# State-space stage of a two-layer decoder: three of four channel blocks summed by accumulating transposes, and a third block convolved on TensorE

## The chip, the cores and the metric

One core of one Trainium2 chip runs the whole program. Its engines are TensorE (PE in the profile, PEld its weight loads), VectorE (DVE), ScalarE (ACT), GpSimd (POOL) and SyncE (SP), which issues the DMAs. The metric is the device time of one launch in microseconds (us), the median over runs.

## What is computed

A decoder of two layers over 8 sequences of 100 tokens and 256 channels. Layer 0 is a gated scan, cross attention and a mixture of experts; layer 1 is four state-space blocks, cross attention and a quantised feed-forward. The change touches the state-space blocks alone. One of the four is, cut:

```python
h = rms(x, norm_w[i])
xz = einsum('bld,ed->ble', h, W_in[i]);  xi, z = split(xz, 2)         # 512 channels each
xc = silu(conv_b[i] + sum(xp[:, k:k + L] * conv_w[i][:, k] for k in range(4)))
dbc = einsum('bld,ed->ble', xc, W_x[i]);  delta, Bm, Cm = split(dbc)
delta = softplus(einsum('blr,dr->bld', delta, W_dt[i]) + b_dt[i])
deltaA = exp(delta[..., None] * A);  BX = (delta * xc)[..., None] * Bm[:, :, None, :]
hs = scan(deltaA, BX)                                                 # 16 states per channel
y = einsum('bldn,bln->bld', hs, Cm) + D[i] * xc
x = x + einsum('bld,ed->ble', y * silu(z), W_out[i])
```

## The kernel before

The state-space stage works in 8 rounds (`ROUNDS`), one for each of 4 blocks and each of 2 groups of four sequences (`GT` = 400 tokens). The 512 channels lie as four blocks c = 0 to 3 of 128 partitions (`CD`), and the 16 states come four at a time, so a round has 16 units (`UNITS`): unit u is block u // 4 and states 4 (u % 4) to 4 (u % 4) + 3, a tile of 128 x 1600. A unit passes through the engines so:

- GpSimd multiplies dx by the rows of B (`gm_bx`, L2003), two units ahead, into one of three buffers.
- ScalarE takes the exponentials of a half unit (128 x 800) into one of two PSUM halves (`am_unit`, L1886). The half that it writes must have been consumed two halves before.
- VectorE scans each half. For eleven units of a round (`DVE_C`) it scans in PSUM (L2089) and multiplies by the rows of C itself (L2092). For units 1, 2, 6, 9 and 12 it scans into SBUF (L2094), and GpSimd multiplies by C (`gm_c`, L2015).
- TensorE adds the four states of a unit onto the sum of the block, four fp32 matmuls with the identity (`pm_reduce`, recorded under the helper's line L675), two units later (`LAG_R`); after the fourth unit of a block one more adds D times xc. The sums lie in banks 4 and 5. VectorE multiplies a block's sum by silu(z) (`vm_y`, L2110).

Between the units, each engine's program holds the side work for the next round, at places given in units by the table `AT`; a piece at u stands behind unit u of its engine. TensorE: output projection of the round before (`pO`), transposes (`pT`, L1547), input projections X0 to X7 (`pX`), convolution of blocks 2 and 3 (`pm_conv`), the product DB (`pB`), steps D0 to D3 (`pD`). ScalarE: squares and scales for the norm (L1756, L1776), copies of T, X, Y, DB (L1787, L1801, L1807, L1825, L1845), the taps as scaled identities for the TensorE convolution in every second round (`am_taps`, L1816), softplus (L1852) and silu (L1835, L1840) with table loads around (L670). VectorE: convolution of blocks 0 and 1 (`vm_conv`, L2052), three steps each. GpSimd: delta (L1992) and the norm's root (L1953 to L1960).

The results of the side work use PSUM banks 6 and 7 in turn, in the order of the list `PREP`; each waits until the one two places before it has been read. Every engine's program is in order, with semaphore waits written by hand. The last round has no next one to prepare; pieces of the following attention stand in it as guests.

Of the kernel before, what the change touches and what calls it, by code (L numbers as in the profile page):

```python
# [17 lines left out]
P = 128  # L18
# [10 lines left out]
G = 2  # L29
# [70 lines left out]
    "aK": 2,  # L100
    "aQ": 4,
    "gN": 4,
    "aH": 5,
    "pT": 7,
    "aT": 6,
    "pX": (9, 9, 8, 8, 15, 15, 16, 16),
    "aG": (5, 6),
    "aX": 7,
    "aY": 8,
    "aC": 9,  # L110
    "vC": 10,
    "aZ": (15, 15, 16, 16),
    "aV": 3,
    "aS": 11,
    "pB": 11,
    "aB": 12,
    "pD": (12, 12, 14, 14),
    "aD": (13, 14),
    "aA": 10,
    "gA": 15,  # L120
    "gD": (14, 15, 19, 21),
    "vY": (5, 10, 13, 16),
# [110 lines left out]
def decoder(nc, inp, out):  # L233
    ctx = ExitStack()
    with ctx:
# [62 lines left out]
        taps = mam.take(2, DC, P)  # L298
        mam.at += CD * GT - 2 * DC * P
        dx = mam.take(CD, GT)  # L300
        bx = mam.take(BX, SEGMENT * GT)
        hs = mam.take(HS, SEGMENT * GT)
        y2 = mam.take(CD, GT)
# [663 lines left out]
        def act_attn(act, a, steps):  # L967
            for g in steps:
# [11 lines left out]
                if a.layer == 0:  # L980
# [41 lines left out]
                    if g == AHEAD["aU"]:  # L1022
                        am_unit(act, 0)
# [372 lines left out]
        m_taps = sem("m_taps")  # L1396
        ROUNDS = G * NL


        PREP = (["T0", "T1", "X2", "X3", "Y2", "Y3", "X0", "X1", "DB"] + [f"D{c}" for c in range(CD)]  # L1400
# [47 lines left out]


# [111 lines left out]

        def pm_conv(pe, m, c):

            pe.wait_ge(m_taps, m // G + 1)
            n = f"Y{c}"
            p_read(pe, m, f"X{c}")
            p_free(pe, m, n)
            y3 = ps[:, p_bank(m, n), 0:GT].rearrange("p (b t) -> p b t", b=GB)
            x3 = xc[m % G][:, c].rearrange("p (b t) -> p b t", b=GB)
            for s in range(DC):  # L1570
                last = mm(y3[:, :, s:S], taps[:, c - 2, DC - 1 - s], x3[:, :, 0:S - s], s == 0, s == DC - 1)
            last.then_inc(m_full, 1)
# [16 lines left out]
        def pm_reduce(pe, unit):  # L1589
# [12 lines left out]
            last.then_inc(m_red, 1)  # L1602

# [71 lines left out]
        def mam_pe(pe):  # L1675
            for m in range(ROUNDS):
                for u in range(UNITS):
# [8 lines left out]
                    if m + 1 < ROUNDS:  # L1686
# [7 lines left out]
                        for e in (0, 1, *range(CD, 2 * CD)):  # L1694
                            if u == AT["pX"][e]:
                                pm_in(pe, m + 1, e)
                    if UNITS * m + u >= LAG_R:
                        pm_reduce(pe, UNITS * m + u - LAG_R)
                    if m + 1 < ROUNDS:
                        if u == AT["pB"]:  # L1700
                            pm_dbc(pe, m + 1)
                        for c in range(CD):
# [69 lines left out]
        def am_scale(act, m, g):  # L1772
# [5 lines left out]
            if m >= 2:  # L1778
                am_keep(act, m - 2, g, 0)
                am_keep(act, m - 2, g, 1)  # L1780
# [29 lines left out]
        def am_taps(act, m, l, c):  # L1810

            act.wait_ge(ld_w, 80 * (l + 1))
            if m and c == 2:
                p_full(act, m, "Y3")
            for k in range(DC):
                last = nc.scalar.activation(taps[:, c - 2, k], ident[:, :], ACT.Identity,  # L1816
                                            scale=cvw[:, DC * c + k:DC * c + k + 1])
            if c == 3:
                last.then_inc(m_taps, 1)
# [7 lines left out]
        def am_silu(act, m, g):  # L1827
# [4 lines left out]
            for names, c in ((("Y2", "Y3"), 2), (("X0", "X1"), 0)):  # L1832
# [35 lines left out]
        def am_unit(act, unit):  # L1868

            m, u = divmod(unit, UNITS)  # L1870
            c, nq = divmod(u, NQ)
            l, g = divmod(m, G)
            if nq == 0:
# [3 lines left out]
            for h in range(2):  # L1877
                k = 2 * unit + h
                if unit:
                    if on_dve(unit - 1):  # L1880
                        act.wait_ge(m_cmd, dve_halves(unit - 1, h))
                    else:
                        act.wait_ge(m_scan, k - 1)
                for j in range(2):
                    n = c * NS + nq * SEGMENT + 2 * h + j
                    last = nc.scalar.activation(psf[:, half_at(k) + j * GT:half_at(k) + (j + 1) * GT],  # L1886
                                                delta[g][:, c], ACT.Exp, scale=aneg[:, l % 2, n:n + 1])
                last.then_inc(m_exp, 1)

        def mam_act(act):  # L1890
            table(act, SET_EXP_LN)
            for m in range(ROUNDS):
                l, g = divmod(m, G)
                ng = 1 - g
                for u in range(UNITS):
                    if m or u:
                        am_unit(act, UNITS * m + u)
                    for c in range(CD):
                        if m and u == AT["aZ"][c] - UNITS:
                            am_z(act, m, g, c)  # L1900
                    if u == AT["aV"]:
                        table(act, SET_SILU)
                        am_silu_z(act, m, g)
                        table(act, SET_EXP_LN)
                    if u == AT["aK"] and g == 0:
                        am_skip(act, m, l)
                    if m + 1 == ROUNDS:
                        if u == AT["aH"]:
                            am_keep(act, m - 1, ng, 0)
                            am_keep(act, m - 1, ng, 1)  # L1910
                        guest_act(act, u)
                        continue
                    if u == AT["aQ"]:
                        am_square(act, m + 1, ng)
                    if u == AT["aH"]:
                        am_scale(act, m + 1, ng)
                    if u == AT["aT"]:
                        am_turned(act, m + 1)
                    for c in (2, 3):
                        if u == AT["aG"][c - 2] and (m == 0 or g == 1):  # L1920
                            am_taps(act, m, l + g, c)
                        if u == AT["aX"]:
                            am_raw_x(act, m + 1, ng, c)
                    for c in (2, 3):
                        if u == AT["aY"]:
                            am_conv_out(act, m + 1, ng, c)
                    for c in range(2):
                        if u == AT["aC"]:
                            am_conv(act, m + 1, ng, c)
                    for c in range(CD):  # L1930
                        if u == AT["aZ"][c]:
                            am_z(act, m + 1, ng, c)
                    if u == AT["aS"]:
                        table(act, SET_SILU)
                        am_silu(act, m + 1, ng)
                        table(act, SET_EXP_LN)
                    if u == AT["aB"]:
                        am_dbc(act, m + 1)
                    for k in range(2):
                        if u == AT["aD"][k]:  # L1940
                            table(act, SET_SOFTPLUS)
                            for c in (2 * k, 2 * k + 1):
                                am_soft(act, m + 1, ng, c)
                            table(act, SET_EXP_LN)
                    if u == AT["aA"] and g == 1:
                        am_rates(act, l + 1)
# [96 lines left out]
        def vm_conv(dve, m, g, c0):  # L2043

            dve.wait_ge(m_acc, 2 * m + CD)
            for s in range(1, DC):
                for c in (c0, c0 + 1):
                    n = f"X{c}"
                    a3 = xc[g][:, c].rearrange("p (b t) -> p b t", b=GB)[:, :, s:S]
# [601 lines left out]
```

## Time and profile before

| | |
|---|---|
| median of 3 runs | 1283.72 us (1283.09 to 1285.94) |
| profiled execution | 1284.21 us, its span 1282.5 us |
| mean granted TensorE clock | 0.955 |
| busy: PE, DVE, ACT, POOL | 1120.2, 1050.9, 824.7, 775.1 us |
| state-space stage, VectorE's first scan to its last y | 359 to 1058 us |
| starts of unit 4 (behind the silu of z) in the rounds from the third on | 556.32, 642.00, 728.85, 814.81, 901.34, 987.03 us |

The last line gives rounds of 85.7, 86.9, 86.0, 86.5 and 85.7 us. Rounds are counted from 0 in what follows; the even one that is read closely runs from 556.3 to 642.0. A line of the timeline has the start, the time to the last end, the engine, the source line, the operation and its shapes, how many instructions are merged, and in brackets the idle time before it and who ended it. Where the engine named had long been done, the wait was another.

### The profile page before, as it was taken

Reading aid. Unit: us, or ns where it says so; the run is one execution under the profiler, and the core shown is the slowest. Engines: PE = TensorE matmul, PEld = TensorE weight load, DVE = VectorE, ACT = ScalarE, POOL = GpSimd, SP = SyncE. Lnnn points to the kernel's source line nnn. Section 1 sums busy time; section 2 is a strip of 40 time slices with the busy share of each in tenths; the row PEclk is TensorE's granted clock in tenths of the full one; section 3 lists DMA queues with packets and bytes.
Section 4 is the critical chain, followed back from the end, with each engine's and each line's share of the span. In section 5 each row is a group of like instructions: output and inputs, shape, how many; then the busy total and the mean of one; then the engine's idle time right before and its main releaser. Section 6 shows DMA issues by size and latency. Waiting matters only on the chain.

```text
span 1282.5 us, 17476 instructions
## 1 busy us (share of the span) xinstructions
PE 1120.2 (87%) x5960; PEld 655.7 (51%) x5960; DVE 1050.9 (82%) x1642; ACT 824.7 (64%) x1816; POOL 775.1 (60%) x641
## 2 busy tenths in 40 slices
PE   7798888888859899999998999999989679999874
PEld 3455555444425454454554544545545336667643
DVE  4567777676598999999999999999999895776667
ACT  1455555655476776776777767867776436788863
POOL 6001111100379889899899898998998961554212
PEclk9899999998789999999999999999999899999988
DMA  7000002000330420501504206005033003010000
GB/s 212 13 13 13 13 13 73 2 1 3 126 120 1 179 73 0 207 17 44 207 1 144 79 1 241 11 12 195 17 123 115 1 1 101 18 34 18 2 2 26
DMA packets 22141, 79.13 MB, mean 62 GB/s; under 512 B 4935, under 2 KB 8847, under 8 KB 21138
## 3 DMA queue, kind: packets, MB, share of 16 engines
q1 hardware_dynamic: 22054, 78.02, 17.5%
q8 instruction: 48, 0.79, 0.3%
q14 instruction: 39, 0.32, 0.1%
HBM read 76.77 MB, written 1.24 MB: 61 GB/s over the span
## 4 chain that ended last, share of the span: by engine, by line
PE 31%; DVE 31%; POOL 22%; issue 7%; ACT 7%; DMA 1%; SPq 0%; DVEq 0%; POOLq 0%; ACTq 0%
PE ps L675 27%; DVE ps L2089 13%; POOL arena L2003 13%; POOL arena L2015 6%; DVE arena L2092 4%; PE ps L744 4%; DVE hstat L1213 2%; DVE arena L2094 2%; DVE arena L2052 2%; DVE arena L1189 1%; POOL arena L1992 1%; ACT ps L1886 1%; ACT arena L936 1%; DMA arena<-in_exb 1%; DVE arena L1179 1%
## 5 line engine op out<-in xcount | busy, mean ns | idle before, releaser
L675 PE MATMUL ps<-arena 128*32 128x100 f32 (+10 forms) x3330 | 513.2, 375 | 54.2 <-ACT arena L936 15.1
L2003 POOL TENSOR_TENSOR arena<-arena 128x1600 f32<-128x1600 f32 x128 | 456.8, 3584 | 30.9 <-DVE ps L2089 22.6
L675 PE MATMUL ps<-arena,ident 128*128 128x400 f32 x1024 | 381.8, 522 | 45.2 <-POOL arena L2015 35.7
L1886 ACT ACTIVATE ps<-arena 128x400 f32<-128x400 f32 x512 | 282.9, 590 | 187.4 <-DVE arena L2092 152.9
L675 PEld LDWEIGHTS ps<-arena 128*32 128x32 f32 (+7 forms) x3330 | 259.1, 143 | 276.5 <-issue 114.3
L2089 DVE TENSOR_TENSOR_SCAN ps<-ps,arena 128x800 f32<-128x800 f32 x176 | 320.8, 1822 | 20.6 <-ACT ps L1886 12.6
L675 PEld LDWEIGHTS ps<-arena,ident 128*128 128x128 f32 x1024 | 198.6, 198 | 210.4 <-POOL arena L2015 44.1
L642 POOL TENSOR_SCALAR stat<-stat 100x1 f32<-100x1 f32 (+1 forms) x44 | 8.5, 193 | 420.0 <-DVE stat L623 419.0
L2092 DVE TENSOR_TENSOR arena<-ps,arena 128x800 f32<-128x800 f32 x176 | 174.4, 991 | 6.0
L2015 POOL TENSOR_TENSOR arena<-arena 128x1600 f32<-128x1600 f32 x40 | 143.1, 3578 | 17.5 <-DVE arena L2094 17.5
L2094 DVE TENSOR_TENSOR_SCAN arena<-ps,arena 128x800 f32<-128x800 f32 x80 | 140.3, 1803 | 2.1 <-ACT ps L1886 1.4
L960 ACT ACTIVATE arena<-ps 128x400 f32<-128x400 f32 x192 | 89.8, 503 | 24.0 <-PE ps L744 23.0
L744 PE MATMUL ps<-ident,arena 100*128 100x100 f32 x768 | 93.2, 259 | 8.1 <-DVE arena L1337 3.6
L951 ACT ACTIVATE arena<-arena,hstat 100x361 f32<-100x361 f32 x128 | 74.9, 588 | 37.1 <-DVE hstat L1189 37.1
L1189 DVE CUSTOM_DVE_ANT_0 arena<-ps,arena 100x361 f32<-100x361 f32 x128 | 60.6, 530 | 44.0 <-PE ps L675 44.0
L936 ACT ACTIVATE arena<-ps,hstat 100x361 f32<-100x361 f32 x128 | 71.7, 562 | 35.7 <-DVE hstat L1213 35.6
L744 PEld LDWEIGHTS ps<-ident,arena 100*128 100x128 f32 x768 | 77.5, 144 | 27.4 <-issue 9.7
L670 ACT ACT_TABLE_LOAD x65 | 83.4, 1283 | 1.2
L1213 DVE TENSOR_REDUCE hstat<-ps 100x2 f32<-100x722 f32 x64 | 57.8, 905 | 26.0 <-PE ps L675 25.7
L675 PE MATMUL ps<-wv,arena 128*128 128x256 f32 (+1 forms) x192 | 53.9, 407 | 4.3 <-DVE arena L1159 3.4
L675 PE MATMUL ps<-arena,wk 128*128 128x361 f32 x128 | 50.4, 522 | 1.5 <-ACT xm L1768 0.8
L1020 ACT ACTIVATE arena<-ps 100x512 f32<-100x512 f32 x32 | 19.1, 598 | 45.7 <-PE ps L675 41.2
(199 smaller groups left out, 1025.2 us busy)
## 6 DMA issues: line engine op xcount, KB each, us to landing
arena<-bc_scratch SPq DMA_DIRECT2D x64, 800.0 KB, 6.5
arena<-in_ctxT SPq DMA_DIRECT2D x16, 361.0 KB, 4.3
arena<-in_w_in SPq DMA_DIRECT2D x4, 1024.0 KB, 4.9
arena<-in_expT SPq DMA_DIRECT2D x1, 2048.0 KB, 13.0
arena<-in_w_out SPq DMA_DIRECT2D x4, 512.0 KB, 3.3
arena<-in_mask SPq DMA_DIRECT2D x8, 141.0 KB
arena<-in_xT SPq DMA_DIRECT2D x2, 400.0 KB, 4.0
x_tok<-in_x_tok SPq DMA_DIRECT2D x1, 800.0 KB
```

What stands on the lines that cost most here:

```text
L670: act.add_instruction(mybir.InstLoadActFuncSet(name=nc.get_next_instruction_name(), act_func_set_id=which, engine=mybir.EngineType.Activat ...
L675: return nc.tensor.matmul(outp, lhsT, rhs, start=first, stop=last)
L744: last = nc.tensor.transpose(ps[:, a.bank(b, name), k * S:(k + 1) * S], a.es[0:S, (n * QUAD + i) % 8, kc * P:(kc + 1) * P], ident[0:S, 0:S])
L936: nc.scalar.activation(a.es[0:S, v % 8, 0:SK], ps[0:S, i, 0:SK], ACT.Exp, bias=hstat[0:S, n % 2, 0, i:i + 1], scale=1.0, accum_out=hstat[0 ...
L960: nc.scalar.activation(a.aT[:, n % 2, r * QUAD * S:(r + 1) * QUAD * S], ps[:, a.bank(b, name), 0:QUAD * S], ACT.Copy).then_inc(a.freed(b, ...
L1213: nc.vector.tensor_reduce(hstat[0:S, n % 2, 0, i:i + 2], ps[0:S, i:i + 2, 0:SK], AX.X, ALU.max, negate=True).then_inc(a.max_ready, 1)
L1886: last = nc.scalar.activation(psf[:, half_at(k) + j * GT:half_at(k) + (j + 1) * GT], delta[g][:, c], ACT.Exp, scale=aneg[:, l % 2, n:n + 1])
L2003: nc.gpsimd.tensor_tensor(bx[:, unit % BX].rearrange("p (j t) -> p j t", j=SEGMENT), bbc[:, nq].rearrange("p (j t) -> p j t", j=SEGMENT), ...
L2015: nc.gpsimd.tensor_tensor(h, h, cbc[:, nq], ALU.mult).then_inc(m_cmp, 1)
L2089: nc.vector.tensor_tensor_scan(a, a, bx[:, unit % BX, w], 0.0, ALU.mult, ALU.add).then_inc(m_scan, 1)
L2092: nc.vector.tensor_tensor(y, a, cbc[:, nq, w], ALU.mult).then_inc(m_cmd, 1)
L2094: nc.vector.tensor_tensor_scan(y, a, bx[:, unit % BX, w], 0.0, ALU.mult, ALU.add).then_inc(m_scan, 1)
```

## The change

- The sums of blocks 0, 1 and 2: a bank is cleared by one matmul of zeros (bf16), and then each of the 16 pieces (four states, four sequences, 128 channels x 100 tokens) is transposed onto it, accumulating, as 100 tokens x 128 channels. ScalarE copies the turned sum to SBUF (`am_turned_sums`), and `pm_back` puts D times xc and four transposes back into the same bank. Block 3 is summed as before.
- Block 1 is convolved on TensorE as well (raw copy, `pm_conv`, biased copy); VectorE keeps block 0, three instructions in place of six.
- Places: the programs of ScalarE and VectorE are now cut by half units. Old side work of ScalarE stays where it was (u is now u + 0.5). The copies of the turned sums (`aYT`), the taps (`aG`) and block 1's raw copy and output take places of their own. The y multiplies move from behind units 5, 10, 13 and 16 to 7.0, 11.5, 15.5 and 16.5. Steps D2 and D3 go ahead of the sum in their step on TensorE. The taps have three semaphore counts in place of one, and `am_keep` is called by itself.

```diff
-    "aG": (5, 6),
+    "aG": {2: 7.0, 3: 8.0, 1: 9.0},
     "pX": (9, 9, 8, 8, 15, 15, 16, 16),
-    "aX": 7, "aY": 8, "aC": 9, "vC": 10, "aS": 11, "aB": 12, "aD": (13, 14), "aA": 10,
+    "aX": 7.5, "aY": 8.5, "aR1": 9.5, "aC": 9.5, "vC": 10.5, "pY1": 10, "aY1": 10.5,
+    "aS": 11.5, "aB": 12.5, "aD": (13.5, 14.5), "aA": 10.0,
+    "aYT": (6.0, 10.5, 15.0),
+    "pY": (7, 11, 15),
+    "vY": (7.0, 11.5, 15.5, 16.5),
...
-        PREP = (["T0", "T1", "X2", "X3", "Y2", "Y3", "X0", "X1", "DB"] + [f"D{c}" for c in range(CD)]
+        PREP = (["T0", "T1", "X2", "X3", "Y2", "Y3", "X1", "X0", "Y1", "DB"] + [f"D{c}" for c in range(CD)]
...
+            if c < CD - 1:
+                if nq == 0:
+                    mm(ps[0:S, 4 + c % 2, :], identb[0:1, 1:S + 1],
+                       identb[0:1, :].rearrange("p (o t) -> p o t", o=1).to_broadcast([1, GB, P]), True, False)
+                for j in range(SEGMENT):
+                    for b in range(GB):
+                        last = nc.tensor.matmul(ps[0:S, 4 + c % 2, b * P:(b + 1) * P],
+                                                hs[:, unit % HS, j * GT + b * S:j * GT + (b + 1) * S], ident[:, :],
+                                                is_transpose=True, start=False,
+                                                stop=nq == NQ - 1 and j == SEGMENT - 1 and b == GB - 1)
+                last.then_inc(m_red, 1)
+                return
...
+        def pm_back(pe, m, c):
+
+            pe.wait_ge(m_yt, (CD - 1) * m + c + 1)
+            pe.wait_ge(m_skip, m // G + 1)
+            o = ps[:, 4 + c % 2, 0:GT]
+            mm(o, dgd[:, c], xc[m % G][:, c], True, False)
+            for b in range(GB):
+                last = nc.tensor.matmul(o[:, b * S:(b + 1) * S], turned_rows(c)[0:S, b * P:(b + 1) * P], ident[0:S, 0:S],
+                                        is_transpose=True, start=False, stop=b == GB - 1)
+            last.then_inc(m_yb, 1)
...
+        def am_turned_sums(act, m, c):
+
+            act.wait_ge(m_red, UNITS * m + NQ * (c + 1))
+            nc.scalar.activation(turned_rows(c)[0:S, :], ps[0:S, 4 + c % 2, :], ACT.Copy).then_inc(m_yt, 1)
...
+                        if u == AT["pY1"]:
+                            pm_conv(pe, m + 1, 1)
+                        for c in (2, 3):
+                            if u == AT["pD"][c]:
+                                pm_dt(pe, m + 1, c)
                     if UNITS * m + u >= LAG_R:
                         pm_reduce(pe, UNITS * m + u - LAG_R)
+                    for c in range(CD - 1):
+                        if u == AT["pY"][c]:
+                            pm_back(pe, m, c)
...
-        def vm_conv(dve, m, g, c0):
-            dve.wait_ge(m_acc, 2 * m + CD)
+        def vm_conv(dve, m, g):
+
+            dve.wait_ge(m_acc, m + CD)
+            n = "X0"
             for s in range(1, DC):
-                for c in (c0, c0 + 1):
...
+            if c < CD - 1:
+                dve.wait_ge(m_yb, (CD - 1) * m + c + 1)
+            else:
+                dve.wait_ge(m_red, UNITS * m + NQ * CD)
             nc.vector.tensor_tensor(y2[:, c], ps[:, 4 + c % 2, 0:GT], sz[g][:, c], ALU.mult).then_inc(m_y2, 1)
```

## Rows read from the trace of the kernel before

**Rows 1.** Windows: span, busy (instructions) of PE, PEld, DVE, ACT, POOL, PEclk, DMA.

```profile
470.00:556.00 86.00, 79.96 (x248) 44.70 (x247) 83.05 (x64) 64.30 (x123) 79.80 (x36) 0.98 0.23 83
556.00:642.00 86.00, 80.82 (x250) 45.29 (x249) 83.08 (x65) 61.98 (x112) 80.22 (x35) 0.98 0.26 94
```

**Rows 2.** Timeline of VectorE in an even round.

```profile
542.81 6.95 DVE L2094 TENSOR_TENSOR_SCAN arena<-ps,arena 128x800 f32<-128x800 f32 x4
...
571.48 1.83 DVE L2089 TENSOR_TENSOR_SCAN ps<-ps,arena 128x800 f32<-128x800 f32 x1
...
592.11 3.54 DVE L2052 SCALAR_TENSOR_TENSOR arena<-ps,arena 128x396 f32<-128x396 f32 x6
...
601.09 3.52 DVE L2094 TENSOR_TENSOR_SCAN arena<-ps,arena 128x800 f32<-128x800 f32 x2
...
610.05 0.57 DVE L2110 TENSOR_TENSOR arena<-ps,arena 128x400 f32<-128x400 f32 x1
...
616.58 1.83 DVE L2089 TENSOR_TENSOR_SCAN ps<-ps,arena 128x800 f32<-128x800 f32 x1 [0.24 <-POOL arena L2003]
...
627.99 0.57 DVE L2110 TENSOR_TENSOR arena<-ps,arena 128x400 f32<-128x400 f32 x1 [0.27 <-PE ps L675]
```

**Rows 3.** Timeline of GpSimd in the same round.

```profile
546.41 3.57 POOL L2015 TENSOR_TENSOR arena<-arena 128x1600 f32<-128x1600 f32 x1 [1.68 <-DVE arena L2094]
...
567.82 7.11 POOL L2003 TENSOR_TENSOR arena<-arena 128x1600 f32<-128x1600 f32 x2
...
592.54 7.14 POOL L2003 TENSOR_TENSOR arena<-arena 128x1600 f32<-128x1600 f32 x2
```

**Rows 4.** Timeline of ScalarE, same round, the exponentials behind the second softplus.

```profile
615.33 2.15 ACT L1886 ACTIVATE ps<-arena 128x400 f32<-128x400 f32 x4
```

**Rows 5.** Timeline of TensorE, same round.

```profile
584.00 2.85 PE L675 MATMUL ps<-arena,ident 128*128 128x400 f32 x8
...
592.65 4.62 PE L675 MATMUL ps<-arena,ident 128*128 128x400 f32 x8 [2.44 <-POOL arena L2015]
...
613.58 2.95 PE L675 MATMUL ps<-arena 128*128 128x400 f32 x8 [0.70 <-ACT arena L1852]
...
621.75 5.54 PE L675 MATMUL ps<-arena,ident 128*128 128x400 f32 x16
627.12 0.83 PE L675 MATMUL ps<-arena 128*128 128x400 f32 x2
```

**Rows 6.** Timeline of VectorE, ahead of unit 7 in rounds 0 and 3.

```profile
398.77 1.83 DVE L2089 TENSOR_TENSOR_SCAN ps<-ps,arena 128x800 f32<-128x800 f32 x1 [1.40 <-ACT ps L1886]
...
658.03 1.83 DVE L2089 TENSOR_TENSOR_SCAN ps<-ps,arena 128x800 f32<-128x800 f32 x1 [0.65 <-ACT ps L1886]
```

**Rows 7.** Transposes on the timeline; windows, one of L744 alone; PEclk third from last.

```profile
651.65 0.85 PE L1547 MATMUL ps<-ident,arena 100*128 100x100 f32 x8
...
55.17 0.87 PE L744 MATMUL ps<-ident,arena 100*128 100x100 f32 x4
...
1130.00:1225.00 95.00, 87.64 (x1063) 62.82 (x1062) 61.14 (x241) 77.43 (x235) 38.19 (x81) 1.00 0.04 13
...
1130.00:1225.00 95.00, 26.33 (x241) 22.82 (x240) 1.00 0.04 13
...
1042.00:1058.00 16.00, 11.88 (x34) 6.21 (x34) 13.39 (x14) 3.34 (x6) 5.09 (x4) 1.00 0.00 0
```

**Rows 8.** Durations: taps, conv (ns, min/median/max), copy of 100x512, matmul of 512 columns.

```profile
L1816 ACT ACTIVATE arena<-ident,arena x32: 388/440/457, 390.8 to 829.3; 128x128 f32<-128x128 f32 x32
...
L2052 DVE SCALAR_TENSOR_TENSOR arena<-ps,arena x42: 611/621/628, 419.6 to 940.1; 128x396 f32<-128x396 f32 x14, 128x392 f32<-128x392 f32 x14, 128x388 f32<-128x388 f32 x14
...
L1020 ACT ACTIVATE arena<-ps 100x512 f32<-100x512 f32 x32 | 19.1, 598 | 45.7 <-PE ps L675 41.2
...
L675 PE MATMUL ps<-arena 3*100 3x512 bf16 x32 | 13.2, 413 | 0.0
```

**Rows 9.** Timeline of VectorE, the last y of the stage.

```profile
1058.35 0.57 DVE L2110 TENSOR_TENSOR arena<-ps,arena 128x400 f32<-128x400 f32 x1 [2.79 <-PE ps L675]
```

More of the change, by code:

```diff
@@ L297, in decoder @@
         delta[1] = mam.take(CD, GT)
-        taps = mam.take(2, DC, P)
-        mam.at += CD * GT - 2 * DC * P
+        taps = mam.take(3, DC, P)
+        mam.at += CD * GT - 3 * DC * P
         dx = mam.take(CD, GT)
@@ L1447, in out_read_wait, with turned_rows @@
             p_read(eng, m, "O1")
+        def turned_rows(c):
+            at = y2_at + min((c + 1) * GT, CD * GT - GB * P)
+            return arena[:, at:at + GB * P]
         def on_dve(u):
@@ L1570, in pm_conv @@
             for s in range(DC):
-                last = mm(y3[:, :, s:S], taps[:, c - 2, DC - 1 - s], x3[:, :, 0:S - s], s == 0, s == DC - 1)
+                last = mm(y3[:, :, s:S], taps[:, c - 1, DC - 1 - s], x3[:, :, 0:S - s], s == 0, s == DC - 1)
             last.then_inc(m_full, 1)
@@ L1701, in mam_pe @@
                             pm_dbc(pe, m + 1)
-                        for c in range(CD):
+                        for c in (0, 1):
                             if u == AT["pD"][c]:
@@ L1866, in am_skip, with am_half @@
             last.then_inc(m_skip, 1)
-        def am_unit(act, unit):
+        def am_half(act, k):
+            unit, h = divmod(k, 2)
             m, u = divmod(unit, UNITS)
@@ L1872, in am_unit @@
             l, g = divmod(m, G)
-            if nq == 0:
+            if nq == 0 and h == 0:
                 act.wait_ge(m_first, CD * m + c + 1)
@@ L1876, in am_unit @@
                     act.wait_ge(m_aneg, l + 1)
[L1877 to L1888, printed above, removed]
+            if k >= 2:
+                before, bh = divmod(k - 2, 2)
+                if on_dve(before):
+                    act.wait_ge(m_cmd, dve_halves(before, bh))
+                else:
+                    act.wait_ge(m_scan, k - 1)
+            for j in range(2):
+                n = c * NS + nq * SEGMENT + 2 * h + j
+                last = nc.scalar.activation(psf[:, half_at(k) + j * GT:half_at(k) + (j + 1) * GT],
+                                            delta[g][:, c], ACT.Exp, scale=aneg[:, l % 2, n:n + 1])
+            last.then_inc(m_exp, 1)
         def mam_act(act):
@@ L1892, in mam_act @@
             for m in range(ROUNDS):
[L1893 to L1946, printed above, removed]
@@ L2094, in vm_half @@
                 nc.vector.tensor_tensor_scan(y, a, bx[:, unit % BX, w], 0.0, ALU.mult, ALU.add).then_inc(m_scan, 1)
-        def vm_unit(dve, unit):
-            wait(dve, m_red, unit - HS + 1)
-            dve.wait_ge(m_bx, unit + 1)
-            for h in range(2):
-                vm_half(dve, unit, h)
         def vm_y(dve, m, c):
@@ L2114, in mam_dve @@
             for m in range(ROUNDS):
-                g = m % G
-                ng = 1 - g
-                for u in range(UNITS):
-                    if m or u:
-                        vm_unit(dve, UNITS * m + u)
-                    if m + 1 == ROUNDS:
-                        guest_dve(dve, u)
+                for k in range(2 * UNITS):
+                    unit, h = UNITS * m + k // 2, k % 2
+                    if m or k >= 2:
+                        if h == 0:
+                            wait(dve, m_red, unit - HS + 1)
+                            dve.wait_ge(m_bx, unit + 1)
+                        vm_half(dve, unit, h)
+                    if m + 1 == ROUNDS and h == 1:
+                        guest_dve(dve, k // 2)
                     for c in range(CD):
-                        if u == AT["vY"][c]:
+                        if k / 2 == AT["vY"][c]:
                             vm_y(dve, m, c)
-                        if m and u == AT["vY"][c] - UNITS:
+                        if m and k / 2 == AT["vY"][c] - UNITS:
                             vm_y(dve, m - 1, c)
-                    if m + 1 < ROUNDS:
-                        if u == AT["vC"]:
-                            vm_conv(dve, m + 1, ng, 0)
+                    if m + 1 < ROUNDS and k / 2 == AT["vC"]:
+                        vm_conv(dve, m + 1, 1 - m % G)
             vm_y(dve, ROUNDS - 1, CD - 1)
```

140 lines of the change are left out of this document (104 added, 36 removed).

## The prediction

> **What bounds the kernel now.** I read the windows by round first. The state-space stage runs from 359 to 1058 us in eight rounds of 16 units. In a round of 86 us VectorE works 83, TensorE 80 to 81, GpSimd 80 and ScalarE 62 to 64 [rows 1]. Three engines stand within 3 us of each other, so an edit to one is worth what the others let through, and the question is which is late in each stretch.
>
> The timeline of a round of the even kind (556.3 to 642.0) answers that. A half unit on VectorE costs 2.78 us where it also multiplies by C (four between 616.58 and 627.72) and 1.74 us where GpSimd does (four in 6.95) [rows 2]. Measured from the end of unit 1 (546.4):
> - Units 2 to 6: GpSimd is late. It runs without a gap from 546.41 (C of unit 1); its first multiply of 567.82 ends at 571.4, and VectorE starts unit 7 at 571.48 [rows 2, 3]. 25.1 us pass, of which VectorE's own units need 23.6 (3 x 5.56 and 2 x 3.48); the first y multiply (0.57 long, 0.5 net) and waits fill the rest.
> - Units 7 to 12: VectorE is late. It never idles; the convolution of two blocks stands here, six instructions in 3.54 us at 592.11 [rows 2].
> - Units 13 and 14: ScalarE is late. Two softplus blocks with table loads lie between its exponentials; the one for unit 15 starts at 615.33 and VectorE, after y of block 2 (610.05) and unit 14, starts at 616.58 with 0.24 idle [rows 2, 4].
> - Unit 15 to the last y: TensorE is late. From 613.58 (X4, X5) it is dense to 627.95 and y of block 3 waits 0.27 for it [rows 2, 5].
>
> Odd rounds (from 470, 642, 815) are 0.9 us longer, since ScalarE writes the taps behind units 5 and 6 there; 0.65 of it stands ahead of unit 7 at 658.03 [rows 6]. Round 0 has the same stall with 1.40 (398.77).
>
> **The convolution.** Six instructions take 3.54 us [rows 2]. Three are left, each dependent on the one before, so they can't overlap: 3 x 0.62 and two hand-overs of 0.04 make 1.94 (0.62 is the length of one [rows 8]). Gain 1.60 in a VectorE-bound stretch, in seven rounds: -11.2. ScalarE's part changes from one scaled copy to a raw copy and a biased copy, about 0.5 more, behind units 9 and 10, where it waits for VectorE in every half. What comes late next, were VectorE quicker there: unit 12 needs GpSimd's product of 592.5 to 596.1 and starts at 601.09 [rows 2, 3], so 1.6 is free to take.
>
> **The moved y multiplies.** y of block 0 leaves the GpSimd-bound stretch, where it was covered, for the VectorE-bound one (after the first half of unit 7). Its 0.5 stops being hidden: 7 x 0.5 = +3.5. In the last round GpSimd binds further on, so nothing there. y of block 1 moves inside one stretch: nothing. y of block 2 leaves the ScalarE-bound stretch, whose length is fixed by ScalarE's chain, for a place behind unit 15, where TensorE is late.
>
> **TensorE.** A unit's sum is now eight records in 2.85 us, sixteen in 5.54, so 2.69 net [rows 5]. The only transposes of this form are 100-column ones, eight in 0.85 us with the last 0.25 long, hence 0.086 apart [rows 7]. The new ones stream 128 columns: 0.086 x 1.28 = 0.110 as an estimate (bounds 0.086, if the weight load sets it, and 0.15, as in the four at 55.17 in 0.87 at half the clock). Sixteen make 1.4 to 2.4, I take 1.75: 0.93 less in each of 12 units, 11 us a round. Added: three clearing matmuls (nearest row 0.41 each with its latency [rows 8]; I take 0.2), three times four transposes back (0.34), a third convolution of 2.7. The matmul with D only moves. Net about 7 us less in a round. But this gain lies where TensorE isn't late. Where it is, units 12 to 15 keep the old sums, and the return of block 2 (D matmul 0.67 and four transposes 0.34) is set into the dense stretch: 613.58 + 14.37 + 1.01 = 628.96, before 627.99. D2 and D3 ahead of the sum of unit 12 save nothing, as X4 must wait for ScalarE to read D2 anyway. With y of block 2 in its new place VectorE alone would be there at 616.58 + 11.07 + 0.5 = 628.15. So block 3's y comes 0.7 to 0.9 later: three even rounds 0.86, three odd ones 0.7 (there D2's wait of 0.3 goes), round 0 0.8: +5.5.
>
> **ScalarE.** The three new copies (100x512) cost about 0.60 each by the nearest row [rows 8]; a set of taps is 4 instructions of 0.44, partly overlapped, 1.32 in all [rows 8]. The first copy falls after the exponentials of unit 6's first half. Worked from unit 1's end in an odd round: exponential 12 ends at 20.7, copy 21.3, exponential 13 22.4 against a use at 22.9; turned rows 23.5, exponential 14 24.6 against 24.9; taps 25.9, exponential 15 27.0 against 28.2; raw copies 27.9, exponential 16 29.0 against 31.0; then taps, two biased copies, taps in three half units with 1.0, 0.4 and 0.3 to spare. No stall is left, but little room. So the taps' stalls go: 3 x 0.87, and 1.4 in round 0: -4.0. The copies of blocks 1 and 2 lie beside waits for VectorE. If the copy took 1.2 instead of 0.6, exponential 14 would be late by 0.3 a round, the bound on that side.
>
> **Last round.** VectorE idles 2.79 ahead of the very last y, for TensorE's sum of the last unit [rows 9]. y of block 2 moves into that wait: -0.5.
>
> **The clock.** With shorter sums TensorE waits more. Before it fell to half (592.65, a unit's sum in 4.62 instead of 2.85) it had idled 2.44 us [rows 5]. In the new kernel it has gaps of 1 to 2 us between the sums of units 2 to 5. If it enters unit 5's sum at 1.2 GHz, the chain sum, return, X2, X3 (5.4 us) ends some 3.5 us later and the exponential of unit 8, which has 2.0 to spare, is late by 1.3. I count that for one round in three: 7 x 0.45 = +3.1 (0 at the one end, 7 x 2.5 = 17.5 with that chain wholly at 1.2 GHz at the other).
>
> The Trainium skill, in "TensorE: Matmul & The Clock Gate", Part 4: PE-mode transpose, says that transposes don't count as TensorE being busy, so that the full clock doesn't engage for them. By it the clock would be low in most of each round. The trace leans against it: from 1130 to 1225 transposes fill 26 of 88 busy us and the clock stays at 1.00 [rows 7]; but matmuls lie between them there, so it is no proof.
>
> **Sum.** -11.2 + 3.5 + 5.5 - 4.0 - 0.5 + 3.1 = -3.6. The profiled execution took 1284.2 us (span 1282.5 and 1.7 around it), 0.5 above the median: 1280.6 for it, 1280.1 for the median. I say 1280.
>
> **Rivals.**
> 1. The moved multiplies cost nothing, since ScalarE and GpSimd run ahead once VectorE is earlier, and the clock holds: -11.2 - 4.0 - 0.5 and perhaps half of the 9 us of y costs, about 1272. For it: VectorE works 83 of 86 us. Against: three of four stretches of the round are bound elsewhere. 15 in 100.
> 2. All is given back: TensorE's dense end of round and GpSimd's run of 25.1 us hold the round at 85.7, only the stalls of odd rounds and round 0 go against 3 us of clock: 1282 to 1285. For it: GpSimd's work isn't touched and is 80 of 86. Against: at unit 12 GpSimd has 5 us of room [rows 2, 3], so VectorE's gain there reaches the next stretch. 17 in 100.
> 3. Slower: TensorE's clock. Its place is the chain from unit 5's sum to X3 in each round; its point is when X3 ends over 2.0 us late; its price, with some 1.3 there in every round and 0.5 at the softplus inputs, is 7 x 1.8 = 12.6 in place of 3.1: +5.9, near 1290. For it: sums of 1.75 us every 5.5 us leave TensorE idle two thirds of the time between units 3 and 5, and the skill's rule. Against: from 1042 to 1058 sums of 2.85 us with idle between them kept the clock at 1.00 [rows 7]. 18 in 100.
> 4. The change doesn't do what it says: a transpose of 128 columns costs 0.15 or more with its weight load, the sums save nothing, the returns come on top: about 1287. 5 in 100.
>
> The forecast (1276 to 1284) gets 45 in 100.
>
> **How the numbers follow.** A measurement tells about 0.2%, 2.6 us, from no change: faster is below 1281.2, slower above 1286.3. Of the forecast's 45, 32 lie below 1281.2 and 13 above; with rival 1 faster is 47, with rival 2 same is 30, rivals 3 and 4 make slower 23. The range 1270 to 1291 takes in all rivals' centres and leaves out the tails of 1 and 3.
>
> **What would show it.** Right: VectorE's convolution three instructions in 1.9 us; no idle at units 6 and 7 of odd rounds; rounds of 85.5 us both kinds; y of block 3 waiting for TensorE by 0.5 to 0.8; sixteen transposes in 1.8 us. Wrong: the granted clock under 0.9 over a whole round, idle ahead of unit 8 behind ScalarE's raw copies (rival 3); rounds under 84.5 (rival 1); a sum over 2.5 us (rival 4).

## The result, and the profile after

| | before | after |
|---|---|---|
| median of 5 runs each, same chip | 1283.72 us (1278.33 to 1285.94) | 1273.52 us (1269.02 to 1274.84) |
| median on a second chip | 1280.6 us (20 runs) | 1273.36 us (7 runs) |
| profiled execution, its span | 1284.21, 1282.5 us | 1274.84, 1273.1 us |
| mean granted TensorE clock | 0.955 | 0.947 |
| up to VectorE's first scan, first to last scan, rest | 359.2, 692.6, 230.7 us | 353.5, 687.7, 231.8 us |

The ratio is 0.992 [0.990, 0.994] on the first chip and 0.9948 [0.9928, 0.9968] on the second: faster, by 10.2 and 7.2 us, where 3.7 had been forecast. Both medians lie below the forecast of 1276 to 1284 and inside the wider range of 1270 to 1291. The last line of the table splits the profiled span. Its middle part, called the stage below, holds all edits.

The page of after, busy time and share (nothing in GpSimd's work changed; VectorE has 12 us less, TensorE 41 less, ScalarE 18 more):

```profile
PE 1079.3 (85%) x6904; PEld 708.9 (56%) x6904; DVE 1039.0 (82%) x1621; ACT 843.1 (66%) x1863; POOL 775.2 (61%) x641
...
L1617 PE MATMUL ps<-ident,arena 128*100 128x128 f32 x1536 | 195.3, 285 | 52.6 <-POOL arena L2077 43.3
```

Two rounds of after, an odd and an even one (columns as in [rows 1]). TensorE works 4 to 5 us less in a round and VectorE 1.5, yet the even round fell from 85.7 to 85.6 only. The odd ones, 86.5 to 86.9 before, take 86.0, 85.6 and 85.5:

```profile
467.31:553.31 86.00, 76.22 (x369) 51.94 (x368) 81.62 (x62) 67.84 (x131) 80.35 (x36) 0.96 0.24 84
553.31:638.89 85.58, 75.68 (x370) 52.03 (x368) 81.41 (x62) 63.24 (x114) 79.96 (x35) 0.96 0.27 95
```

VectorE's timeline in the even round, where it waits and where it was edited. It now waits where it hadn't in [rows 2]: 0.58 for GpSimd ahead of unit 7 (564.39), 0.59 for ScalarE ahead of unit 14 (602.38), 0.90 for TensorE at y of block 3 (620.76; 0.27 before):

```profile
564.39 1.83 DVE L2149 TENSOR_TENSOR_SCAN ps<-ps,arena 128x800 f32<-128x800 f32 x1 [0.58 <-POOL arena L2065]
...
567.17 0.56 DVE L2167 TENSOR_TENSOR arena<-ps,arena 128x400 f32<-128x400 f32 x1
...
584.89 1.94 DVE L2113 SCALAR_TENSOR_TENSOR arena<-ps,arena 128x396 f32<-128x396 f32 x3
...
602.38 1.83 DVE L2149 TENSOR_TENSOR_SCAN ps<-ps,arena 128x800 f32<-128x800 f32 x1 [0.59 <-ACT ps L1933]
...
608.24 1.83 DVE L2149 TENSOR_TENSOR_SCAN ps<-ps,arena 128x800 f32<-128x800 f32 x1 [0.23 <-POOL arena L2065]
...
620.76 0.57 DVE L2167 TENSOR_TENSOR arena<-ps,arena 128x400 f32<-128x400 f32 x1 [0.90 <-PE ps L682]
```

TensorE's timeline of the same round. A sum of sixteen transposes (L1617) takes 1.95 us, a return is the D matmul and four transposes (L1638), and from 605.42 on the return of block 2 (611.46) stands in the dense stretch:

```profile
550.02 3.70 PE L1617 MATMUL ps<-ident,arena 128*100 128x128 f32 x32 [1.32 <-POOL arena L2077]
...
555.27 1.95 PE L1617 MATMUL ps<-ident,arena 128*100 128x128 f32 x16
560.43 3.42 PE L1617 MATMUL ps<-ident,arena 128*100 128x128 f32 x16 [1.05 <-DVE arena L2152]
...
564.71 8.17 PE L682 MATMUL ps<-arena 128*128 128x400 f32 x24
...
599.39 1.61 PE L682 MATMUL ps<-arena 64*128 64x400 f32 x4 [1.92 <-ACT arena L1899]
600.93 4.65 PE L682 MATMUL ps<-arena,ident 128*128 128x400 f32 x8
605.42 2.85 PE L682 MATMUL ps<-arena 128*128 128x400 f32 x8
...
610.79 0.83 PE L682 MATMUL ps<-arena 128*128 128x400 f32 x2
611.46 0.51 PE L1638 MATMUL ps<-ident,arena 100*128 100x100 f32 x4
```

**The stage by stretches.** From the starts of VectorE's scans on the timelines I took, for each round, the time between the first scans of units 0, 4, 7, 12, 15 and of the next unit 0, and added it up over the rounds. All kernels that were run, in us (the last half unit, 2.8 in each, is in the sum):

| kernel | 0 to 4 | 4 to 7 | 7 to 12 | 12 to 15 | 15 to next 0 | stage |
|---|---|---|---|---|---|---|
| before (three profiles) | 160.2 to 160.4 | 128.5 to 128.6 | 237.1 | 124.6 to 125.1 | 38.8 | 692.2 to 692.6 |
| after (two profiles) | 166.6 | 124.2 to 124.3 | 228.6 to 228.8 | 123.2 | 42.1 | 687.4, 687.7 |
| e2, old sums | 161.5 | 124.1 | 229.0 | 123.7 | 38.8 | 679.8 |
| e3, old convolution | 169.0 | 123.9 | 240.9 | 123.2 | 42.1 | 701.9 |
| e4, taps early | 172.6 | 129.0 | 228.6 | 123.2 | 42.1 | 698.2 |
| e6, blocks 0 and 1 turned | 161.4 | 124.2 | 230.7 | 123.7 | 38.8 | 681.6 |
| e12, the kernel of e6 again | 162.3 | 123.8 | 230.6 | 123.7 | 38.8 | 681.9 |
| e7, block 2 turned | 165.5 | 124.0 | 228.9 | 123.2 | 42.1 | 686.5 |
| e8, taps early, held | 164.8 | 129.4 | 228.2 | 123.2 | 42.1 | 690.5 |
| e9, no D in block 2 | 161.8 | 124.3 | 229.0 | 123.2 | 42.1 | 683.3 |
| e10, held | 165.5 | 123.8 | 228.2 | 123.2 | 42.1 | 685.7 |

The stage repeats within 0.4 us between executions and chips, so parts of a microsecond can be read from it, which no median here allows. Single stretches repeat less well: round 0 takes 21.6 us from unit 0 to 4 in some executions and 22.4 in others of one kernel, and gives 0.4 of that back in the next stretch (e6 and e12). The stretch ahead of the stage, whose work the change leaves alone, doesn't repeat: 355.7 to 359.2 in three profiles of before, 348.2 to 362.5 in those of the changed kernels.

### The profile page after: what moved, and what is told of

Same layout as the page of the kernel before. It is cut to its first block, busy times and chain, and to the rows that moved or that the text cites. A ratio compares the mean times of both kernels' runs of the same rounds, so it can differ in the third digit from the quotient of the medians.

```text
span 1273.1 us, 19421 instructions
## 1 busy us (share of the span) xinstructions
PE 1079.3 (85%) x6904; PEld 708.9 (56%) x6904; DVE 1039.0 (82%) x1621; ACT 843.1 (66%) x1863; POOL 775.2 (61%) x641
## 4 chain that ended last, share of the span: by engine, by line
POOL 46%; PE 28%; DVE 16%; issue 6%; ACT 4%; DMA 1%; SPq 0%; DVEq 0%; POOLq 0%; ACTq 0%
POOL arena L2065 30%; PE ps L682 24%; POOL arena L2077 11%; DVE ps L2149 4%; PE ps L751 3%; DVE hstat L1221 2%; POOL arena L2054 2%; DVE arena L1197 1%; ACT arena L943 1%; DMA arena<-in_exb 1%; DVE arena L1187 1%; DVE arena L2152 1%; ACT arena L958 1%; DVE arena L2449 1%; DVE arena L2426 1%
## 5 line engine op out<-in xcount | busy, mean ns | idle before, releaser
L682 PE MATMUL ps<-arena 128*32 128x100 f32 (+12 forms) x3386 | 541.8, 382 | 57.2 <-ACT arena L1899 15.6
L682 PEld LDWEIGHTS ps<-arena 128*32 128x32 f32 (+9 forms) x3386 | 272.6, 146 | 266.2 <-issue 108.2
L1617 PE MATMUL ps<-ident,arena 128*100 128x128 f32 x1536 | 195.3, 285 | 52.6 <-POOL arena L2077 43.3
L1617 PEld LDWEIGHTS ps<-ident,arena 128*100 128x100 f32 x1536 | 176.7, 134 | 77.7 <-POOL arena L2077 49.3
L682 PE MATMUL ps<-arena,ident 128*128 128x400 f32 x256 | 100.6, 546 | 2.9 <-POOL arena L2077 2.9
L682 PEld LDWEIGHTS ps<-arena,ident 128*128 128x128 f32 x256 | 52.4, 208 | 47.6 <-issue 17.1
```

The costliest lines, as they stand in the source:

```text
L682: return nc.tensor.matmul(outp, lhsT, rhs, start=first, stop=last)
L1617: last = nc.tensor.matmul(ps[0:S, 4 + c % 2, b * P:(b + 1) * P], hs[:, unit % HS, j * GT + b * S:j * GT + (b + 1) * S], ident[:, :], is_tr ...
```

## The experiments

My theory after the result: the stage is worth 4.9 us, made of the terms of the sum; the third convolution on TensorE brings all of it, the turned sums are a cost, and what the medians show beyond 4.9 is the spread of the rest. The rivals: the changed program also makes the rest faster; the turned sums are needed to make room on TensorE for the third convolution; the late y of block 3 is TensorE's length in one reading and its clock in the other.

**e1, the changed kernel again**, no edit.

> The changed kernel once more, for its spread. In the profiled pair the attention and mixture stages ahead of the state-space stage, which the change doesn't touch, took 353.5 us instead of 359.2, and the state-space stage 687.7 instead of 692.6 (first scan to last scan). Theory A: the front's 5.7 us are chance (TensorE's clock falls at other points in each execution); then the front here may lie anywhere from 353 to 359, and the stage again at 686 to 690. Theory B: the change moves the front too; then it is 353 to 354 again.

Measured: stage 687.4 against 687.7, stretch ahead 358.5 against 353.5; median 1273.36. The 5.7 us that the first pair of profiles shows ahead of the stage are not a property of the kernel.

**e5 and e11, the kernel before again**, no edit.

> The kernel before once more, for a second profile of it. The changed kernel's stage came out at 687.7 and 687.4 us in two profiles while its front, which no edit touches, was 353.5 and 358.5. Theory A (the front is chance, the stage is the kernel's): here the stage is 692.6 within 1 us, the front anywhere from 349 to 359. Theory B (the change moves the front): the front is 357 to 361 again.

> The kernel before, a third profile. Theory A (the stretch ahead of the state-space stage, whose work the change does not touch, varies between executions of either kernel by where TensorE's clock falls): stage 692.2 to 692.6 again, front anywhere in 348 to 363. Theory B (the changed program also shortens the front): front 355 to 360 as in both profiles of before, against a median of 352 over the changed kernels.

Measured: stage 692.2 and 692.6; ahead of it 355.7 and 358.6. Both theories on e11 allow 358.6. Eleven profiles of changed kernels have a median of 351.4 there, three of before 358.6, so the question that e11 was to settle stays open (below).

**e2, the third convolution on TensorE with the old sums.**

```diff
-            if c < CD - 1:
+            if False:
                 if nq == 0:
                     mm(ps[0:S, 4 + c % 2, :], ...
...
-    "vY": (7.0, 11.5, 15.5, 16.5),
+    "vY": (5.5, 10.5, 13.5, 16.5),
```

> The changed kernel with the sums as before (four fp32 matmuls a unit, no turned copies, no return), and with the y multiplies where they were; the third convolution on TensorE and the new places of the taps stay. Theory A, my terms: only the terms -11.2 (convolution) and -4.0 (taps) are left, and the costs +3.5 and +5.5 of the moved y multiplies and +3.1 of the clock go: about 15 us under before, 1269, which is some 5 us under the changed kernel; the stage 677 to 679. Theory B: the turned sums are what makes room for the third convolution on TensorE, which without them works 83 of 86 us: then it is slower than the changed kernel, 1278 to 1290, and VectorE shows waits for TensorE or for ScalarE's raw copies.

Measured: 1266.74 us (1265.99 to 1270.17), ratio 0.990 [0.9885, 0.9915], stage 679.8. On the same chip after has 1273.36. So the turned sums cost 6.6 us in the medians and 7.7 in the stage, though TensorE is busier without them. Over 520 us of rounds (columns as in [rows 1]) of e2, and then of after:

```profile
440.00:960.00 520.00, 500.28 (x1588) 283.73 (x1587) 501.91 (x376) 392.68 (x730) 489.85 (x211) 1.00 0.25 91
```

```profile
440.00:960.00 520.00, 458.00 (x2225) 311.86 (x2224) 493.50 (x371) 396.54 (x741) 484.32 (x208) 0.97 0.25 90
```

TensorE works 500 of 520 us in the faster kernel and 458 in the slower one. VectorE's timeline of e2, y of block 3 in an even round, and the scan ahead of unit 10 in an odd one:

```profile
488.28 1.83 DVE L2149 TENSOR_TENSOR_SCAN ps<-ps,arena 128x800 f32<-128x800 f32 x1 [0.88 <-ACT ps L1933]
...
612.59 0.57 DVE L2164 TENSOR_TENSOR arena<-ps,arena 128x400 f32<-128x400 f32 x1 [0.27 <-PE ps L682]
```

The wait for TensorE is back at 0.27. The odd rounds and round 0 of e2 keep a stall of 0.9 from the taps, which has only moved from unit 7 to unit 10, and so its stage is above the 677 to 679 of theory A; in after the same taps find VectorE 0.5 later behind y of block 0. The edit takes back the places of the y multiplies together with the sums; turned sums with other places were not tried.

**e3, the turned sums with the old convolution.**

```diff
-        PREP = (["T0", "T1", "X2", "X3", "Y2", "Y3", "X1", "X0", "Y1", "DB"] + ...
+        PREP = (["T0", "T1", "X2", "X3", "Y2", "Y3", "X0", "X1", "DB"] + ...
...
             for s in range(1, DC):
+                for c in (0, 1):
```

> The changed kernel with blocks 0 and 1 convolved on VectorE as before (six instructions) and one set of taps less; turned sums and all places stay. Theory A: VectorE is late where its convolution stands, so all of 7 x 1.60 = 11.2 us comes back: stage 699, ratio to before 1.000. Theory B: GpSimd or ScalarE hold the round in any case: under 5 us come back, ratio 0.996 or lower.

Measured: 1291.07 us (1284.07 to 1292.06), ratio 1.0067 [1.0048, 1.0085], slower than before; stage 701.9. In "7 to 12" it is 12.2 above after, 1.74 for each of seven rounds, where 1.60 had been the price. Most of the rest of the 14.4 is in "0 to 4": y of block 3 waits 2.54 in rounds 1 and 2, and 0.83 in round 0, where after has 2.55; the other 0.8 is how round 0 was entered. Stage and ratio are above theory A's 699 and 1.000.

```profile
539.81 0.58 DVE L2164 TENSOR_TENSOR arena<-ps,arena 128x400 f32<-128x400 f32 x1 [2.54 <-PE ps L682]
```

**e6, blocks 0 and 1 turned, block 2 summed as before, and e7, block 2 alone turned.** The two parts of what e2 takes away.

```diff
-            if c < CD - 1:
+            if c in (0, 1):
-    "vY": (7.0, 11.5, 15.5, 16.5),
+    "vY": (7.0, 11.5, 13.5, 16.5),
```

> The changed kernel with block 2 summed as before: no turned copy and no return of block 2, its y behind unit 13 again; blocks 0 and 1 stay turned. Theory A: the term +5.5 of my sum goes, the later y of block 3 (0.8 in each of seven rounds); the stage falls from 687.5 to 682, and the wait ahead of the y of block 3 from 0.90 to 0.27. Theory B: the 7.7 us between the changed kernel and the one with the old sums come from blocks 0 and 1; then the stage stays above 686.

```diff
-            if c < CD - 1:
+            if c in (2,):
-    "vY": (7.0, 11.5, 15.5, 16.5),
+    "vY": (5.5, 10.5, 15.5, 16.5),
```

> The changed kernel with blocks 0 and 1 summed as before and their y behind units 5 and 10; block 2 alone is turned. Theory A: the term +3.5 goes (y of block 0 is again beside GpSimd's run): 7 x 0.5, the stage falls from 687.5 to 684, and VectorE's wait of 0.58 for GpSimd ahead of unit 7 goes. Theory B: only the late y of block 3 costs; then the stage stays at 687.

Measured: stages 681.6 and 686.5, 1.8 and 6.7 above e2; 8.5 together, against 7.7 for all three blocks. So block 2 is the dear one. Its cost has two halves of the same size in each round. y of block 2 now stands behind unit 15: "15 to next 0" is 3.4 longer, 0.48 in each of seven rounds, and its leaving "12 to 15" gives back only 0.5 in all, that of the last round (after 123.2, e2 123.7), as ScalarE is late there. And y of block 3 waits 0.6 longer. e6 has neither, but for one wait of 0.90 in round 4; its "7 to 12" has the 0.5 a round of y of block 0, with the stall of the taps of odd rounds hidden, and 2.0 more in the last round, where VectorE waits for a return:

```profile
610.48 0.57 DVE L2167 TENSOR_TENSOR arena<-ps,arena 128x400 f32<-128x400 f32 x1 [0.27 <-PE ps L682]
...
1011.26 0.57 DVE L2167 TENSOR_TENSOR arena<-ps,arena 128x400 f32<-128x400 f32 x1 [1.91 <-PE ps L1638]
```

e7 came out at theory B's 687 and not at theory A's 684, though the wait for GpSimd ahead of unit 7 did go, as A said: its odd rounds had 0.9 more than expected, the stall at unit 10 that e2 has too, and with it y of block 0 in its old place saves next to nothing.

**e12, e6 timed.**

> The kernel with turned sums in blocks 0 and 1 only, third block convolved on TensorE, now timed. From its stage of 681.6 in the profile against 679.8 for old sums in all blocks: theory A (stage alone decides): 1.8 above the old sums' 1266.7, so 1268.5, ratio 0.991 of before. Theory B (its single time of 1263.9 was no chance, the turned sums give something outside the stage): 1264, ratio 0.987.

Measured: 1267.56 us (1264.84 to 1274.24, 6 runs) against 1282.13 (11 runs), ratio 0.9896 [0.9865, 0.9926]; stage 681.9. Theory A's 1268.5 is nearer than 1264, but the interval holds both ratios, 0.991 and 0.987. e6 and e12 can't be told from e2 by time.

**e9, without D times xc in the return of block 2** (that term is left out of the result).

```diff
-            mm(o, dgd[:, c], xc[m % G][:, c], True, False)
+            if c != 2:
+                mm(o, dgd[:, c], xc[m % G][:, c], True, False)
```

> The changed kernel without the matmul of D times xc in the return of block 2 (D of block 2 is left out of the result; the four transposes back stay and the first of them starts the bank). Everything else as in the kernel after. Theory A (the return of block 2 is priced by its length in TensorE's dense end of round): 0.67 us shorter there in every round, so y of block 3 waits about 0.2 instead of 0.83 to 0.90, and where TensorE goes at half clock once, about 1.9. Stage 687.5 - 7 x 0.67 = 682.8 (682 to 684). Theory B (what the turned block 2 costs is ScalarE's copy and the late y of block 2, not TensorE's length): stage 686.5 to 687.5, the wait of y of block 3 under 0.3 but VectorE waiting for ScalarE by as much more.

Measured: stage 683.3, 4.3 less than after, and y of block 3 waits 0.16 to 0.23 (1.87 in round 0 against 2.55):

```profile
531.24 0.57 DVE L2168 TENSOR_TENSOR arena<-ps,arena 128x400 f32<-128x400 f32 x1 [0.16 <-PE ps L682]
```

0.67 us taken off TensorE shortens the wait by 0.67: the end of the round is TensorE's, by the full length of this instruction.

**e4, the first two taps back at their old places.**

```diff
-    "aG": {2: 7.0, 3: 8.0, 1: 9.0},
+    "aG": {2: 5.5, 3: 6.5, 1: 9.0},
```

> The changed kernel with the taps of blocks 2 and 3 back behind units 5 and 6. Theory A: the stalls ahead of unit 7 in rounds 1, 3 and 5 and in round 0 come back, 3 x 0.87 + 1.4 = 4.0 us more than the changed kernel. Theory B: since VectorE now waits 0.6 us for GpSimd ahead of unit 7 in every round, most of the stall is covered: 1 to 2 us more.

Measured: stage 698.2, 10.7 above after where 4.0 was expected; 1281.57 us (1277.58 to 1285.05), ratio 0.9998 [0.9984, 1.0013]. The odd rounds stall ahead of units 6 and 7, and then y of block 3 waits 2.55 in each of them and in round 0, 0.90 in the other even ones:

```profile
472.64 3.54 DVE L2154 TENSOR_TENSOR_SCAN arena<-ps,arena 128x800 f32<-128x800 f32 x2 [0.69 <-ACT ps L1933]
477.32 1.83 DVE L2149 TENSOR_TENSOR_SCAN ps<-ps,arena 128x800 f32<-128x800 f32 x1 [1.14 <-ACT ps L1933]
...
535.33 0.57 DVE L2167 TENSOR_TENSOR arena<-ps,arena 128x400 f32<-128x400 f32 x1 [2.55 <-PE ps L682]
```

In the table "4 to 7" is 4.7 longer, as expected (4.0); "0 to 4" is 6.0 longer, 3 x 1.65 = 4.95 of that is the wait of y of block 3, and 0.8 how round 0 was entered. Neither had been in a theory. e8 and e10 ask what it is.

**e8, e4 with step D1 computed four times, and e10, the changed kernel with it.** The extra matmuls fill TensorE's gaps ahead of D2 and D3.

```diff
+            for _ in range(3 if c == 1 else 0):
+                mm(ps[:, p_bank(m, n), 0:GT], w_dt[0:RK, c * P:(c + 1) * P], dbc[0:RK, :], True, True)
             mm(ps[:, p_bank(m, n), 0:GT], w_dt[0:RK, c * P:(c + 1) * P], dbc[0:RK, :], True, True).then_inc(...)
```

> The kernel with the taps behind units 5 and 6 (stage 698.2), with step D1's matmul issued four times in place of once, so that TensorE works through the gap ahead of steps D2 and D3. Its y of block 3 waited 2.55 us in rounds 0, 1, 3 and 5 and 0.90 in the others. Theory A: the 1.65 more are TensorE at half its clock in the sum of unit 12 and the projection behind it, after the gap; the wait is 0.90 in every round and the stage shorter by 4 x 1.65 = 6.6, 691.6. Theory B: the 1.65 are order (a late release of a bank); the extra work changes nothing or adds to the wait.

> The changed kernel with step D1 computed four times in each round (three extra matmuls of 0.67 us at full clock, into the same bank, ahead of the real one, so TensorE has no long gap before unit 12's sum); the result is the same. Theory A (the one long wait of y of block 3, 2.55 us in round 0, is TensorE at half clock in the sum of unit 12 and X4, X5 after its gap): that wait becomes 0.83 to 0.90, rounds from the first on as in the kernel after, stage 687.5 - 1.65 = 685.8. Theory B (that wait in round 0 comes from something of round 0 itself, such as X4 waiting for ScalarE's softplus): the wait stays 2.5 and the stage 687.4 to 687.7.

Measured: y of block 3 waits 0.83 in rounds 0 to 6 of both; stages 690.5 (7.7 below e4) and 685.7 (1.9 below after). The mechanism can be read on TensorE's timeline at the end of round 0. After:

```profile
426.16 2.29 PE L682 MATMUL ps<-arena 64*128 64x400 f32 x4 [1.92 <-ACT arena L1899]
428.38 5.61 PE L682 MATMUL ps<-arena,ident 128*128 128x400 f32 x8
433.83 2.85 PE L682 MATMUL ps<-arena 128*128 128x400 f32 x8
```

e10:

```profile
426.29 1.61 PE L682 MATMUL ps<-arena 64*128 64x400 f32 x4
427.83 2.95 PE L682 MATMUL ps<-arena,ident 128*128 128x400 f32 x8
432.12 2.95 PE L682 MATMUL ps<-arena 128*128 128x400 f32 x8 [1.34 <-ACT arena L1901]
```

Windows of after at the ends of rounds 0 and 2, and of e10 at the end of round 0 (PEclk third from last):

```profile
427.00:434.00 7.00, 7.00 (x12) 3.28 (x11) 6.31 (x6) 6.93 (x10) 6.94 (x4) 0.52 0.93 303
601.00:604.00 3.00, 3.00 (x6) 1.67 (x6) 2.41 (x2) 2.97 (x6) 3.00 (x2) 0.50 0.85 224
```

```profile
425.00:432.00 7.00, 5.79 (x25) 3.21 (x23) 6.35 (x5) 6.93 (x11) 6.94 (x5) 1.00 0.92 327
```

In e10 the sum of unit 12 takes 2.95 and X4 then waits 1.34 for ScalarE to read D2. In after the clock is at half from 426.9 to 433.8, behind a gap of 1.92 ahead of D2 and D3 (426.16): the sum takes 5.61 instead of 2.95, and X4 starts 1.7 later. In the even round above the clock was at half from 601.0 to 604.4 only and just the sum was slow (600.93, 4.65): that used up the 1.34 and some more, and the y came 0.90 late instead of 0.83. So a fall of 3.4 us fits ahead of X4's other wait and costs 0.07, and one of 6.8 us costs 1.7. The odd rounds of e4 have the long one (512.7 to 519.5 is the first). Adding useless matmuls made the stage shorter in two profiles; neither kernel was timed. Of the 1.9 of e10, the wait of y of block 3 gives 1.7; the rest is 0.45 at unit 10 of round 1 (below) less the entry of round 0.

## Why the prediction was right or wrong

Direction and sign of every term held. The sum was -3.6, all of it in the stage, where -4.9 was measured; the medians moved by -10.2 and -7.2, and the part beyond the stage has no term in the prediction (below). By its own steps, from the table of stretches:

- **Convolution and y of block 0** ("7 to 12"): -11.2 + 3.5 = -7.7 said, -8.4 measured, or -9.0 without the clock's part below. The three instructions take the forecast 1.94 (584.89). Even rounds went from 29.61 to 27.93 in e2 and 28.36 in after, so 1.68 a round instead of 1.60, and 0.43 given back by the y instead of 0.5. That y had been covered where it stood: VectorE now waits 0.58 for GpSimd there (564.39) and unit 7 starts no earlier.
- **Taps** ("4 to 7"): -4.0 said, -4.3 measured. Odd rounds lost their 0.87, round 0 lost 1.9, not 1.4. The sign "no idle at units 6 and 7" held for the taps alone: VectorE waits 0.56 for GpSimd ahead of unit 7 in odd rounds too. e4 confirms the size: back in their old places they cost 4.7 in that stretch.
- **The late end of the round** ("12 to 15", "15 to next 0", "0 to 4"): +5.5 - 0.5 said, +7.8 with the clock and +6.1 without it measured. The text put it as one delay of TensorE, 1.01 of added work against 627.99. It is 0.48 for y of block 2 behind unit 15 and 0.68 on average for the longer wait of y of block 3, 1.16 in each of seven rounds where 0.8 was said, less 0.5 in rounds 0, 3 and 4 and 0.5 in the last round. The 0.5 of rounds 0, 3 and 4 also went in e2, and a second profile of before (e5) has it in 0 and 4 only; whether the place of D2 and D3, which I had said saves nothing, or the clock gave it was not tried alone.
- **The clock**: +3.1 said, for unit 5's sum and the copies behind it; measured about 2.2, three quarters of it elsewhere. Unit 5's sum did run at half clock in rounds 1 to 3 (560.43, 3.42 instead of 1.95), and TensorE was back at full speed right behind it (564.71, 24 records in 8.17). The step that failed is the 3.5 us of delay that I took it to have: the sum alone is 1.5 longer. In the even round no scan came late by it. In round 1 it reached VectorE not at unit 8 but at unit 10, which waited for the sum of unit 7:

```profile
474.42 3.40 PE L1617 MATMUL ps<-ident,arena 128*100 128x128 f32 x16 [1.06 <-DVE arena L2152]
```

```profile
493.77 1.83 DVE L2149 TENSOR_TENSOR_SCAN ps<-ps,arena 128x800 f32<-128x800 f32 x1 [0.34 <-PE ps L1617]
```

  "7 to 12" took 28.81 in that round and 28.49 in round 3, against 28.34 to 28.36 in rounds 0, 2 and 4 to 6; in e10, whose clock stayed at 1.00 there, round 1 has 28.36. That is 0.6 in all. The greater price, 1.65, fell at the end of round 0 (2.55 against 0.90). The Trainium skill, in "TensorE: Matmul & The Clock Gate", Part 4: PE-mode transpose, had spoken for a low clock in most of each round. The runs disagree: with three of four sums made of transposes the granted clock over 520 us was 0.97, against 1.00 with none (e2). A difference of 0.03 is there, but whether the transposes or TensorE's longer gaps make it was not separated.
- **Sixteen transposes** 1.75 said; 1.95 with the latency of the last, and (3.70 - 1.95) / 16 = 0.109 apart, as estimated. TensorE lost 4 to 5 us a round and not 7, part of it by the half clock, and this bought nothing, as the text held: the saving lies at units 0 to 11, where TensorE isn't late.

By stretch -8.4 + 6.1 - 4.3 + 1.7 = -4.9 (the 0.6 of the clock at unit 10 is in the -8.4). The forecast of rounds of 85.5 of both kinds held (85.5 to 86.0 from the second on); rounds under 84.5 came only without turned sums in block 2 (e2, e6, e12).

The median of 1273.5 lies nearer to rival 1's 1272 than to 1280, yet rival 1's mechanism is not what happened: two of the three moved multiplies were paid for (0.43 a round for block 0, 0.48 for block 2; block 1 cost nothing, as said). So the nearness to 1272 is chance in part, from the spread outside the stage. Rivals 3 and 4 are out by the clock and by the length of the sums; rival 2 named the right stretches, but the convolution's gain outweighed them.

**What is left over** is the rest of the 10.2. Medians less stage, each against before (stage 692.6):

| | median | stage | difference |
|---|---|---|---|
| after, first chip | -10.2 | -4.9 | -5.3 |
| after, second chip | -7.2 | -5.2 | -2.0 |
| e2 | -13.9 | -12.8 | -1.1 |
| e3 | +10.5 | +9.3 | +1.2 |
| e4 | +1.0 | +5.6 | -4.6 |
| e12 | -14.6 | -10.7 | -3.9 |

Work outside the stage is the same in all, and the difference runs from +1.2 to -5.3, with a mean of -2.6. Most of that is the spread of the stretch ahead of the stage. Its length goes with the clock granted in it, whichever kernel runs: at 0.93 it took 359.2 and 358.6 in before and 358.5 in the changed kernel (e1), at 0.94 355.7 in before (e5), at 0.95 to 0.96 348.2 to 354.6 in nine profiles of changed kernels, at 0.92 362.5 (e8). TensorE is busy for 303.7, 303.9 and 303.8 us in the three at 0.93, so its work isn't shorter after the change. Whether the changed programs meet the higher clock there more often (nine of eleven profiles, none of three of before) or this is chance stays open; e11 didn't settle it, and nothing I ran names a cause. The prediction had no term for it and no width for it but that of the rivals.

## What to carry to other kernels

Work taken from the busiest engine is worth nothing where that engine isn't late: with the sums turned TensorE works 458 of 520 us instead of 500, and the stage is 7.7 us longer, most of it because the return and the later y of block 2 landed in the one stretch where TensorE is late. Price a moved instruction twice, for the cover that it leaves and for the queue that it joins. And split the span into the stretch that the edits touch and the rest before explaining a median: here the stretch with the edits repeated within 0.4 us, the one ahead of it moved by 14.

## What the hardware showed that was not expected

- Transposes of fp32 accumulate in PSUM, sixteen onto each place of a cleared bank; 128 x 100 onto 100 x 128 pieces followed each other 0.109 us apart at full clock and sixteen took 3.42 behind a gap, at half clock, instead of 1.95; the clearing matmul of 512 bf16 columns took 0.39 to 0.41 with its latency.
- A gap of 1.92 us ahead of two short steps was followed by 2.29 and 5.61 us for work of 1.61 and 2.95. Three extra matmuls that fill it, 2.0 us of work, kept the clock at 1.00 there and removed 1.9 us from the stage.
- The same gap didn't always have the same fall behind it: D2 and D3 took 1.61 in round 2 and 2.29 in round 0, with the clock at half for 3.4 and for 6.8 us.
